# Low parts of queries and keys on GpSimd from SBUF, two GpSimd additions and four denominator groups a half, scratch laid out in tiles

## Chip, core and metric

The kernel runs on one core of a Trainium2 chip. The metric is the device time of one execution in microseconds, as the median of several runs. The engines are TensorE (PE in the profile, its weight loads PEld), VectorE (DVE), ScalarE (ACT), GpSimd (POOL) and SyncE (SP, which only issues DMAs here).

## What is computed

A gated block: attention of the normalised `x` over a context that is both keys and values, added to `x` through a gate, and then a feed-forward part with values rounded to 16 bits and weights to 4.

```python
q = q * cos + rotate_half(q) * sin            # q = layernorm(x), k = v = ctx_1024
k = k * cos + rotate_half(k) * sin            # B, T, H = 4, 1024, 512; 16 heads of 32
bias = alibi_slopes(nh)[:, None, None] * rel.astype(q.dtype)
scores = jnp.einsum('bqhd,bkhd->bhqk', q, k) * scale + bias[None]
out = jnp.einsum('bhqk,bkhd->bqhd', jax.nn.softmax(scores, axis=-1), v)
...
x = act_qdq(x)                                # rounds by one scale for the whole tensor
up = act_qdq(x @ lpbq_dequant(w_up).T)        # w_gate, w_up: (1536, 512); w_down: (512, 1536)
gate = act_qdq(x @ lpbq_dequant(w_gate).T)
gate = act_qdq(gate * fixed_qdq_u16(jax.nn.sigmoid(gate)))
o = act_qdq(gate * up)
return o @ lpbq_dequant(w_down).T
...
x = x + jnp.tanh(g_xattn[0]) * _L0_xattn_ref(_layernorm(x), ctx_1024, ctx_1024, 16)
x = x + jnp.tanh(g_ffn[0]) * _L0_ffn_ref(_layernorm(x), w_gate, w_up, w_down)
```

## The kernel before

The program is written out engine by engine: each engine has a function that issues its instructions in a fixed order, and semaphores tie the engines together. `STEPS`, a list of `Step` objects, is the order of the attention for all five engines; nothing is scheduled by a tool.

**Attention.** Four heads of one batch are worked on at a time, 16 such quads. A quad has two halves of 512 queries (`hf`, 0 to 31), and a half has eight steps (`s`), one for each 128 keys. In this text `w` is 8 times the half in its quad plus `s`, 0 to 15, and `p` is the quad. In each step:

- TensorE computes the scores of four heads (`score`, L934), the scores of ten steps later once more in the other direction to find row maxima (`row_max`, L921), and the products of the exponentials of the step before with the values (L983). Each is four matmuls side by side in the array, one for each 32 columns.
- ScalarE takes the exponentials of four heads (L1145), out of two PSUM banks in turn, so TensorE can be only two heads ahead. They go to `Pb`, a ring of `NP` = 6 buffers. Between them, or behind them in the step, ScalarE has `numT` (step 1, L1176), `denT` (step 3, L1182), high parts (L1123), normalised tiles (L1095), and later weights.
- VectorE reduces two score tiles of 1024 columns to row maxima (L1348), out of two double banks (`quad`) in turn. The order of their uses is `UNIT_USES`: a use waits until that of two places before is read.
- GpSimd rotates queries and keys (`rope`, L1781 to L1799, three parts in three steps) and adds exponentials.

**Denominators.** The sum over keys is made of eight tiles of exponentials. In each half GpSimd adds tiles 0 and 1, tiles 3 and 4, and tiles 6 and 7 (`sum`, L1936) into `Ps[0]`, `Ps[2]` and `Ps[1]`; two DMAs that accumulate, issued by GpSimd, add tile 2 to `Ps[0]` and tile 5 to `Ps[2]` (`accumulate`, L1915). TensorE multiplies the three sums with ones (`denominators`, L956): group 0 in step 6, groups 1 and 2 in steps 1 and 2 of the next half. The last half is done otherwise: VectorE adds pairs, and there are four groups.

**Low parts.** Queries and keys are split into two half-precision numbers each. ScalarE writes the high part into `S` from the rotated `t1`. For the low part ScalarE copies `t1` into a bank of `quad` (`copy_part`, L1129), which is one more use of these, and VectorE subtracts the high part from it (`low_part`, L1367) at `w` = 1, 6, 10 and 14. When both are there, SyncE issues a transposing DMA (`load_stack`) into `QA` or `KA`.

**Feed-forward part.** Gate and up projections run on TensorE; ScalarE copies each tile of 128 x 1024 out of PSUM, and SyncE stores it into `gate_scratch` or `up_scratch` in HBM, laid out (12, 128, 4096) (L784). They are loaded back when the scale of the whole tensor is known: `load_gate` for the gate beside the up projection, `load_product` for the maximum of the product after it, and `load_o` in halves of 512 columns beside the down projection.

Of the kernel before, what the change touches and what calls it, by code (L numbers as in the profile page):

```python
# [15 lines left out]
N = B * T  # L16
# [12 lines left out]
NXL, NWL, NWQ, NP = 7, 4, 2, 6  # L29
# [86 lines left out]
class Step:  # L116


    def __init__(self, g):
# [109 lines left out]
def unit_uses():  # L229

    uses = []
    for st in STEPS:
# [4 lines left out]
        if st.low is not None:  # L237
            uses.append(("part", *st.low))
# [25 lines left out]
def den_no(hf, n):  # L264

    return 3 * hf + n + 1


def sum_no(hf, n):

    return 3 * hf + (1, 3, 2)[n]
# [56 lines left out]
class Kernel:  # L328


    def __init__(self, nc, ctx, x, ctx_in, gx, gf, wg, wu, wd, cos_d, sin_d, id_d, bias_d, out):
# [9 lines left out]
        self.gate_d = nc.dram_tensor("gate_scratch", (OT, 128, N), F32).ap()  # L341
        self.up_d = nc.dram_tensor("up_scratch", (OT, 128, N), F32).ap()
# [45 lines left out]
        self.Pb = [A(f"P{i}", [128, 4, 512], F32) for i in range(NP - 1)]  # L388
        self.bias = nc.alloc_sbuf_tensor_at("bias", [32, T], F32, offset=A.at - 2 * 8192)
        self.biasT = A("biasT", [128, 8, 4, 16], F16)  # L390
        self.Ps = [A(f"Ps{i}", [128, 4, 512], F32) for i in range(3)]
# [32 lines left out]
        self.Pb.append(A("P5", [128, 4, 512], F32))  # L424
# [87 lines left out]
        self.a_cp = sem("a_cp")  # L512
# [10 lines left out]
    def bank_release(self, use, half):  # L523

        n = UNIT[use] - 2
        while n >= 0:
# [3 lines left out]
            if kind == "out":  # L530
                return (self.v_x2 if half else self.v_rec), a[0] + 1
            if half == 0:
                return self.v_lo, part_no(*a)
            n -= 2
# [97 lines left out]
def sync_program(e, K):  # L632
# [22 lines left out]
    def load_stack(p, w, half):  # L655
# [10 lines left out]
        e.wait_ge(K.v_lo, part_no(p, w, half))  # L666
# [113 lines left out]
    def store_projection(n, dst_d):  # L780
# [3 lines left out]
        e.dma_start(dst_d[ot, :, 1024 * cp:1024 * cp + 1024], K.ev[k % NEV][:, :]).then_inc(K.d_ev[k % NEV], 16)  # L784
# [31 lines left out]
    def load_gate(n):  # L816
# [5 lines left out]
        e.dma_start(K.gt[n % NGT][:, :], K.gate_d[ot, :, GW * cp:GW * cp + GW]).then_inc(K.d_gt[n % NGT], 16)  # L822
# [26 lines left out]
    def load_up(ot, sl, w):  # L849
# [7 lines left out]
        e.dma_start(K.uf[n % NUF][:, 0:w], K.up_d[ot, :, sl]).then_inc(K.d_uf[n % NUF], 16)  # L857
# [1152 lines left out]
```

## Time and profile before

| | us |
|---|---|
| median of 3 runs | 1798.62 |
| lowest and highest | 1795.56, 1801.59 |
| the profiled execution | 1800.73 |
| its span, first to last instruction | 1798.9 |

| engine | busy us | share of the span |
|---|---|---|
| TensorE | 1605.8 | 89% |
| VectorE | 1479.7 | 82% |
| ScalarE | 1241.8 | 69% |
| GpSimd | 838.6 | 47% |

The attention takes the time up to about 900 us, gate and up projection run until about 1440 us, the maximum of the product is searched until 1547 us, and then the down projection runs to the end.

How to read it: in a timeline a row has the start in us from the first instruction, the duration, the engine, the line, the operation, what it writes and reads, shapes, and how many instructions were merged; brackets give the idle time before it and what ended it. A merged row's duration spans all of it. A product in single precision counts as two matmuls. In the table of stretches each engine has its busy time and, in parentheses, its instructions, in the order PE, PEld, DVE, ACT, POOL; then follow TensorE's granted clock as a share of full speed, the busy share of the DMA engines and GB/s. Busy shares of engines that wait for each other do not add up; what sets the end has to be read from the order of events.

### The profile page before, as it was taken

What the parts mean: (1) busy time and instruction counts of PE and PEld (TensorE: products, weight loads), DVE (VectorE), ACT (ScalarE), POOL (GpSimd) and SP (SyncE); (2) the same over time, 40 slices, a digit from 0 to 9 for tenths busy, and PEclk for the clock granted to TensorE, in tenths of its full rate; (3) what the DMA queues carried; (4) which work ended last, traced back from release to release, by engine and by line L of the source; (5) the groups of instructions that cost most, each with busy time, mean ns of one, the idle gap of its engine ahead of it and who ended that gap; (6) DMA issues with size and microseconds to landing.
All of it is one profiled execution on the core that took longest, in us unless ns stands there. A gap on an engine that the chain in (4) does not pass through costs nothing. (4 is left out here: it accounts for less than half of the span.)

```text
span 1798.9 us, 36886 instructions
## 1 busy us (share of the span) xinstructions
PE 1605.8 (89%) x14777; PEld 633.3 (35%) x14777; DVE 1479.7 (82%) x2116; ACT 1241.8 (69%) x1974; POOL 838.6 (47%) x504
## 2 busy tenths in 40 slices
PE   3899999999999999999869999999999900699999
PEld 0233333333333333333224444444444400344444
DVE  7899999999998898898569989768889998854551
ACT  3688888888889899888723323359986699844440
POOL 5699999999999999998600100200000000000000
PEclk9999999999999999999979999999999955899999
DMA  6688888988888887776649888569973479755551
GB/s 153 151 154 179 167 164 180 177 164 167 163 173 161 171 183 151 163 151 136 139 117 275 242 250 239 203 194 284 280 226 127 139 250 302 237 189 172 176 168 61
DMA packets 344204, 331.73 MB, mean 184 GB/s; under 512 B 214849, under 2 KB 273601, under 8 KB 336097
## 3 DMA queue, kind: packets, MB, share of 16 engines
q1 hardware_dynamic: 335104, 264.37, 55.2%
q0 software_dynamic: 8928, 65.02, 18.3%
q8 instruction: 116, 1.90, 0.4%
q14 instruction: 56, 0.45, 0.1%
HBM read 136.77 MB, written 76.55 MB: 119 GB/s over the span
## 5 line engine op out<-in xcount | busy, mean ns | idle before, releaser
L1348 DVE TENSOR_REDUCE cm<-quad 128x1 f16<-128x1024 f32 x512 | 600.3, 1214 | 63.3 <-PE quad L921 62.3
L1145 ACT ACTIVATE P<-quad 128x512 f32<-128x512 f32 x1024 | 556.8, 598 | 112.3 <-PE quad L934 100.5
L1936 POOL TENSOR_TENSOR Ps<-P,P 128x2048 f32<-128x2048 f32 x93 | 441.0, 4742 | 43.2 <-ACT P L1145 43.1
L934 PE MATMUL quad<-QA,KA 101*32 101x512 f16 x4096 | 365.9, 385 | 6.8 <-ACT P L1145 5.3
L921 PE MATMUL quad<-KA,QA 100*32 100x512 f16 x4096 | 334.7, 391 | 35.6 <-DMA QA<-S 17.8
L983 PE MATMUL quad<-P,cg 128*32 128x512 f32 x2048 | 265.5, 594 | 0.0
L1010 PE MATMUL quad<-x_hl,Wu 128*128 128x512 f16 x1152 | 250.8, 381 | 3.4 <-DMA Wu<-wt_scratch 3.4
L1010 PE MATMUL quad<-x_hl,Wg 128*128 128x512 f16 x1152 | 249.3, 379 | 3.1 <-DMA x_hl<-xs 2.5
L1063 PE MATMUL quad<-Wd,oh 128*128 128x512 f16 x768 | 228.6, 379 | 0.0
L934 PEld LDWEIGHTS quad<-QA,KA 101*32 101x32 f16 x4096 | 105.0, 94 | 298.6 <-ACT P L1145 231.0
L1226 ACT ACTIVATE ev<-quad 128x1024 f32<-128x1024 f32 x96 | 97.3, 1014 | 123.4 <-PE quad L1010 117.3
L921 PEld LDWEIGHTS quad<-KA,QA 100*32 100x32 f16 x4096 | 106.4, 96 | 176.1 <-DVE cm L1348 78.2
L1010 PEld LDWEIGHTS quad<-x_hl,Wu 128*128 128x128 f16 x1152 | 113.0, 98 | 141.0 <-DMA Wu<-wt_scratch 4.3
L1010 PEld LDWEIGHTS quad<-x_hl,Wg 128*128 128x128 f16 x1152 | 112.4, 98 | 140.0 <-issue 5.0
L1618 DVE TENSOR_REDUCE mxt<-ev 128x1 f32<-128x1024 f32 x96 | 116.5, 1214 | 39.6 <-ACT ev L1226 39.3
L1063 PE MATMUL quad<-Wd,ol 128*128 128x512 f16 x384 | 145.5, 379 | 0.0
L1883 POOL TENSOR_TENSOR wq<-wl,wsc 128x512 f32<-128x512 f32 x36 | 43.9, 1221 | 216.5 <-DVE wl L1486 216.5
L1257 ACT ACTIVATE sgm<-gq,qs 128x1024 f32<-128x1024 int16 x96 | 110.0, 1147 | 38.1 <-DVE sgq L1663 36.6
L956 PE MATMUL quad<-Ps,ones 128*32 128x512 f32 x776 | 101.9, 600 | 17.1 <-POOL Ps L1936 7.2
L1759 DVE SCALAR_TENSOR_TENSOR xr<-quad,qs,xr 128x512 f32<-128x512 f32 x32 | 23.9, 750 | 112.3 <-PE quad L1063 108.0
L1063 PEld LDWEIGHTS quad<-Wd,oh 128*128 128x128 f16 x768 | 75.1, 98 | 90.7 <-DVE ol L1738 0.2
L1016 PE MATMUL quad<-ident,column 128*128 128x128 f32 x3 | 1.4, 457 | 110.9 <-DVE column L1421 110.9
(167 smaller groups left out, 2006.3 us busy)
## 6 DMA issues: line engine op xcount, KB each, us to landing
Ps<-P POOLq DMA_DIRECT2D x62, 1024.0 KB, 8.1
gate_scratch<-ev SPq DMA_DIRECT2D x48, 512.0 KB, 3.8
gt<-gate_scratch SPq DMA_DIRECT2D x48, 512.0 KB, 5.8
up_scratch<-ev SPq DMA_DIRECT2D x48, 512.0 KB, 3.4
uf<-up_scratch SPq DMA_DIRECT2D x48, 512.0 KB, 5.1
uf<-up_scratch SPq DMA_DIRECT2D x96, 256.0 KB, 3.6
wt_scratch<-wh SPq DMA_DIRECT2D x72, 128.0 KB, 2.8
xl<-in_x_dram SPq DMA_DIRECT2D x32, 256.0 KB, 5.1
```

Of the source, the lines that this page charges most:

```text
L921: mm = e.matmul(K.bank(use, c)[j:j + 32, :], K.QA[p % 2][0:100, 4 * qc + qt, h, j:j + 32], K.KA[p % 2][0:100, 4 * c:4 * c + 4, h, :], star ...
L934: mm = e.matmul(K.score[h % 2][j:j + 32, :], K.KA[p % 2][0:101, kt, h, j:j + 32], K.QA[p % 2][0:101, 4 * qc:4 * qc + 4, h, :], start=True, ...
L956: mm = e.matmul(K.den[32 * h:32 * h + 32, :], K.ones[:, :], K.Ps[n % 2 if hf == NHALF - 1 else n][:, h, :], start=n == 0, stop=n == (3 if ...
L983: mm = e.matmul(K.num[32 * h:32 * h + 32, :], K.cg[(p + 1) % 4][:, kt, 32 * h:32 * h + 32], K.Pb[before.g % NP][:, h, :], start=kt == 0, s ...
L1010: mm = e.matmul(K.quad[z][:, 512 * h:512 * h + 512], W(part, c), K.x_hl[:, x, c0:c0 + 512], start=n == 0, stop=n == 11)
L1063: mm = e.matmul(ps, o[k][:, ot, sl], K.Wd[r][:, ot, :], start=ot == m == 0, stop=ot == OT - 1 and m == 2)
L1145: e.activation(K.Pb[pb][:, h, :], K.score[h % 2], ACT.Exp, scale=SCALE / (QPOW * KPOW)).then_inc(K.a_exp, 1)
L1226: e.activation(K.ev[k % NEV][:, :], K.quad[k % 4][:, :], ACT.Copy).then_inc(K.a_ev, 1)
L1257: e.activation(K.sgm[n % NSG][:, :], view(n), ACT.Sigmoid, scale=sg).then_inc(K.a_sig, 1)
L1348: e.tensor_reduce(cm[:, col:col + 1], K.quad[UNIT["max", hm, u] % 2][:, :], AX.X, ALU.max).then_inc(K.v_max, 1)
L1618: e.tensor_reduce(K.mxt[:, col:col + 1], K.ev[k % NEV][:, :], AX.X, ALU.max, apply_absolute_value=True).then_inc(K.v_mx, 1)
L1936: e.tensor_tensor(K.Ps[n][:, :, :], K.Pb[(st.g - 1) % NP][:, :, :], K.Pb[st.g % NP][:, :, :], ALU.add).then_inc(K.g_sum, 1)
```

## The change

- The low parts of quads 1 to 15 are subtracted by GpSimd, from `t1` and `S` in SBUF. ScalarE's copy and VectorE's subtraction go, and the use of a `quad` bank with them. They stand at `w` = 1, 7, 11 and 15.
- GpSimd adds tiles 0 and 1 and tiles 3 and 4. Tiles 6 and 7 are not added: TensorE reads them as groups of their own. Group 0 (`Ps[0]`) stands in step 6, groups 1 and 2 (tiles 6 and 7) in step 7 and in step 0 of the next half, group 3 (`Ps[1]`) in its step 2.
- `Pb` has seven buffers, since tiles 6 and 7 are read later; `Ps` has two.
- `gate_scratch` and `up_scratch` are laid out (12, 4, 128, 1024), so a tile is one contiguous piece.

```diff
-NXL, NWL, NWQ, NP = 7, 4, 2, 6
+NXL, NWL, NWQ, NP = 7, 4, 2, 7
...
-            elif w in ((10, 14) if p >= 0 else (14, 15)):
-                self.low = (p + 2, 1, w // (14 if p >= 0 else 15))
+            elif w in ((11, 15) if p >= 0 else (14, 15)):
+                self.low = (p + 2, 1, w // 15)
...
-            if w in (1, 6):
-                self.low = (p + 1, 0, w // 6)
+            if w in (1, 7):
+                self.low = (p + 1, 0, w // 7)
...
-        self.sum = (hf, s // 2) if last and s % 2 == 1 else (hf, {1: 0, 4: 2, 7: 1}[s]) if inside and s % 3 == 1 else None
+        self.sum = (hf, s // 2) if last and s % 2 == 1 else (hf, s // 4) if inside and s in (1, 4) else None
...
-        if s == 6 and inside:
-            self.dens = (hf, 0)
-        elif s in (1, 2) and 1 <= hf < NHALF:
-            self.dens = (hf - 1, s)
+        if s in (6, 7) and inside:
+            self.dens = (hf, s - 6)
+        elif s in (0, 2) and 1 <= hf < NHALF:
+            self.dens = (hf - 1, 2 + s // 2)
...
-        if st.low is not None:
-            uses.append(("part", *st.low))
...
-        self.gate_d = nc.dram_tensor("gate_scratch", (OT, 128, N), F32).ap()
-        self.up_d = nc.dram_tensor("up_scratch", (OT, 128, N), F32).ap()
+        self.gate_d = nc.dram_tensor("gate_scratch", (OT, N // GW, 128, GW), F32).ap()
+        self.up_d = nc.dram_tensor("up_scratch", (OT, N // GW, 128, GW), F32).ap()
...
-        else:
-            if n == 1:
-                e.wait_ge(K.g_sum, sum_no(hf, n))
-            else:
-                e.wait_ge(K.d_acc[n // 2], 16 * hf + 16)
+            src = K.Ps[n % 2]
+        elif n in (1, 2):
+            e.wait_ge(K.a_exp, score_no(hf, n + 5, 3))
+            src = K.Pb[(8 * hf + n + 5) % NP]
+        else:
+            e.wait_ge(K.d_acc[n // 3], 16 * hf + 16)
+            src = K.Ps[n // 3]
...
-    def copy_part(p, w, half):
-        use = ("part", p, w, half)
-        e.wait_ge(K.g_rope, rope_no(p, w))
-        e.wait_ge(*K.bank_release(use, 0))
-        e.activation(K.bank(use, 0), K.t1[w][:, 4 * half:4 * half + 4, :].rearrange("t i c -> t (i c)"), ACT.Copy).then_inc(K.a_cp, 1)
...
+    def low_part(p, w, half):
+        rows = slice(4 * half, 4 * half + 4)
+        dst = K.S[w][:, rows, :, :, :].rearrange("t i h n d -> t (i h) n d")
+        src = K.t1[w][:, rows, :].rearrange("t i (h d) -> t (i h) d", d=HD)
+        e.wait_ge(K.g_rope, rope_no(p, w))
+        e.wait_ge(K.d_st[w][half], stack_no(p - 1))
+        e.wait_ge(K.a_hi, part_no(p, w, half))
+        e.tensor_tensor(dst[:, :, 2 - w, :], src, dst[:, :, 0, :], ALU.subtract).then_inc(K.g_lo, 1)
...
-            e.wait_ge(K.g_sum, sum_no(hf, 2 * n))
-            e.dma_start(K.Ps[2 * n][:, :, :], K.Pb[(8 * hf + kt) % NP][:, :, :], accum_op=ALU.add).then_inc(K.d_acc[n], 16)
+            e.wait_ge(K.g_sum, sum_no(hf, n))
+            e.dma_start(K.Ps[n][:, :, :], K.Pb[(8 * hf + kt) % NP][:, :, :], accum_op=ALU.add).then_inc(K.d_acc[n], 16)
+        if st.low is not None:
+            low_part(*st.low)
...
-        e.dma_start(dst_d[ot, :, 1024 * cp:1024 * cp + 1024], K.ev[k % NEV][:, :]).then_inc(K.d_ev[k % NEV], 16)
+        e.dma_start(dst_d[ot, cp, :, :], K.ev[k % NEV][:, :]).then_inc(K.d_ev[k % NEV], 16)
```

TensorE from the end of step 7 to step 2 of the next half, before. L956 is a group of denominators, L934 scores, L921 row maxima, L983 values; the digit behind a name is the buffer, so `Ps1_99` is `Ps[1]`, and one row of x4 is one group:

```order
L983 MATMUL quad3<-P3_94,cg2_86 32x512 x4
L934 MATMUL quad2<-QA1_88,KA1_90 32x512 x8
...
L934 MATMUL quad2<-QA1_88,KA1_90 32x512 x4
L956 MATMUL quad3<-Ps1_99,ones_77 32x512 x4
L983 MATMUL quad3<-P4_95,cg2_86 32x512 x4
L934 MATMUL quad2<-QA1_88,KA1_90 32x512 x8
...
L983 MATMUL quad3<-P5_142,cg2_86 32x512 x4
L956 MATMUL quad3<-Ps2_100,ones_77 32x512 x4
```

and with the change, from step 6 to step 2:

```order
L988 MATMUL quad3<-P1_92,cg2_86 32x512 x4
L961 MATMUL quad3<-Ps0_98,ones_77 32x512 x4
...
L988 MATMUL quad3<-P2_93,cg2_86 32x512 x4
L961 MATMUL quad3<-P2_93,ones_77 32x512 x4
...
L988 MATMUL quad3<-P3_94,cg2_86 32x512 x4
L961 MATMUL quad3<-P3_94,ones_77 32x512 x4
...
L988 MATMUL quad3<-P4_95,cg2_86 32x512 x4
L937 MATMUL quad2<-QA1_88,KA1_90 32x512 x8
...
L988 MATMUL quad3<-P5_142,cg2_86 32x512 x4
L961 MATMUL quad3<-Ps1_99,ones_77 32x512 x4
```

Groups that read `P2` and `P3`, the tiles 6 and 7 of this half, now follow the values in steps 7 and 0, and step 1 has none any more.

GpSimd from the last part of a rotation (step 6) to the first accumulating DMA of the next half, before:

```order
L1799 TENSOR_TENSOR t10_136<-t10_136,t2_138 128x1024
L1936 TENSOR_TENSOR Ps1_99<-P0_91,P1_92 128x2048
L1781 TENSOR_TENSOR t11_137<-cg0_84,cos_75 128x1024
L1936 TENSOR_TENSOR Ps0_98<-P2_93,P3_94 128x2048
L1788 TENSOR_TENSOR t2_138<-cg0_84,sin_76 128x32x16
L1789 TENSOR_TENSOR t2_138<-cg0_84,sin_76 128x32x16
L1915 DMA Ps0_98<-P4_95 128x2048
```

and with the change (L1803 is the low part, `S1` of keys, `S0` of queries):

```order
L1794 TENSOR_TENSOR t10_136<-t10_136,t2_138 128x1024
L1803 TENSOR_TENSOR S1_140<-t11_137,S1_140 128x16x32
L1776 TENSOR_TENSOR t11_137<-cg0_84,cos_75 128x1024
L1803 TENSOR_TENSOR S0_139<-t10_136,S0_139 128x16x32
L1942 TENSOR_TENSOR Ps0_98<-P3_94,P4_95 128x2048
L1783 TENSOR_TENSOR t2_138<-cg0_84,sin_76 128x32x16
L1784 TENSOR_TENSOR t2_138<-cg0_84,sin_76 128x32x16
L1919 DMA Ps0_98<-P5_142 128x2048
```

The sum of 2048 elements between two parts of rotations is gone, and low parts of 512 stand before and behind the first part.

## Rows read from the trace of the kernel before

**Rows 1.** Stretches of time: length, then busy us (x instructions) by engine, clock, DMA.

```profile
200.00:400.00 200.00, 194.44 (x2664) 68.46 (x2664) 187.80 (x263) 172.35 (x322) 187.35 (x107) 1.00 0.84 168
600.00:800.00 200.00, 191.84 (x2616) 67.21 (x2608) 176.10 (x235) 179.11 (x338) 200.00 (x99) 1.00 0.79 161
1200.00:1300.00 100.00, 100.00 (x465) 45.37 (x464) 83.81 (x118) 90.36 (x87) 0.00 (x0) 1.00 0.92 276
```

**Rows 2.** Timeline of ScalarE: start us, duration us, instruction; three `numT` copies.

```profile
113.64 0.71 ACT L1176 ACTIVATE numT<-quad,tg 128x512 f32<-128x512 f32 x1
...
833.31 0.69 ACT L1176 ACTIVATE numT<-quad,tg 128x512 f32<-128x512 f32 x1
...
884.07 0.69 ACT L1176 ACTIVATE numT<-quad,tg 128x512 f32<-128x512 f32 x1
```

**Rows 3.** Timeline of TensorE in halves 10 and 11; in brackets: idle before, and releaser.

```profile
326.24 1.06 PE L956 MATMUL quad<-Ps,ones 128*32 128x512 f32 x8 [0.47 <-POOL Ps L1936]
...
334.18 0.78 PE L934 MATMUL quad<-QA,KA 101*32 101x512 f16 x8
...
338.08 0.61 PE L934 MATMUL quad<-QA,KA 101*32 101x512 f16 x8
...
340.76 0.60 PE L934 MATMUL quad<-QA,KA 101*32 101x512 f16 x8
...
343.43 1.04 PE L956 MATMUL quad<-Ps,ones 128*32 128x512 f32 x8
344.28 0.62 PE L934 MATMUL quad<-QA,KA 101*32 101x512 f16 x8
...
348.52 0.40 PE L921 MATMUL quad<-KA,QA 100*32 100x512 f16 x4 [0.25 <-DVE cm L1348]
```

**Rows 4.** Waits (us, times) before denominator matmuls; landing of the accumulating DMAs, from their lines.

```profile
  DMA Ps<-P: 7.1, 9
...
DMA to landing us min/median/max: 6.8/8.1/10.9
```

**Rows 5.** Timeline of ScalarE, then of VectorE, around two steps 1.

```profile
323.28 1.06 ACT L1123 ACTIVATE S<-t 128x1024 f16<-128x1024 f32 x1
324.23 1.08 ACT L1145 ACTIVATE P<-quad 128x512 f32<-128x512 f32 x2
...
350.71 1.08 ACT L1145 ACTIVATE P<-quad 128x512 f32<-128x512 f32 x2
...
353.20 1.09 ACT L1123 ACTIVATE S<-t 128x1024 f16<-128x1024 f32 x1
...
348.97 2.35 DVE L1348 TENSOR_REDUCE cm<-quad 128x1 f16<-128x1024 f32 x2
351.23 0.68 DVE L1556 TENSOR_REDUCE rmn<-x2s 128x4 f32<-128x512 f32 x1
```

**Rows 6.** Groups by line and form: count, busy us and mean ns, idle before.

```profile
L1367 DVE SCALAR_TENSOR_TENSOR S<-quad,S 128x512 f16<-128x512 f32 x60 | 41.3, 688 | 4.5 <-ACT quad L1129 3.6
...
L1129 ACT ACTIVATE quad<-t 128x512 f32<-128x512 f32 x60 | 36.8, 613 | 17.6 <-DVE cm L1348 17.6
...
L1889 POOL TENSOR_TENSOR wh<-wq,wh 128x512 f16<-128x512 f32 x12 | 20.2, 1686 | 0.0
```

**Rows 7.** Timeline of GpSimd from sum 0 to its accumulating DMA.

```profile
354.20 4.64 POOL L1936 TENSOR_TENSOR Ps<-P,P 128x2048 f32<-128x2048 f32 x1
358.80 1.28 POOL L1788 TENSOR_TENSOR t<-xn,sin 128x512 f32<-128x512 f32 x1
...
361.27 0.76 POOL L1915 DMA_DIRECT2D Ps<-P  x1
```

**Rows 8.** Waits from 1450 to 1545 us; then DMA issues: count, KB, us to landing.

```profile
ACT oh L1296 <- DMA uf<-up_scratch: 5.2, 6, 1.7
...
uf<-up_scratch SPq DMA_DIRECT2D x96, 256.0 KB, 3.6
...
xr<-x_scratch SPq DMA_DIRECT2D x32, 256.0 KB, 3.0
```

More of the change, by code:

```diff
@@ L264, in den_no, with low_no @@
 def den_no(hf, n):
-    return 3 * hf + n + 1
+    return 4 * hf + n + 1
 def sum_no(hf, n):
-    return 3 * hf + (1, 3, 2)[n]
+    return 2 * hf + n + 1
+def low_no(p, w, half):
+    return part_no(p - 1, w, half)
 def rope_no(p, w):
@@ L387, in __init__ @@
         self.KA = [A(f"KA{i}", [128, 8, 4, 128], F16) for i in range(2)]
-        self.Pb = [A(f"P{i}", [128, 4, 512], F32) for i in range(NP - 1)]
+        self.Pb = [A(f"P{i}", [128, 4, 512], F32) for i in range(5)]
         self.bias = nc.alloc_sbuf_tensor_at("bias", [32, T], F32, offset=A.at - 2 * 8192)
         self.biasT = A("biasT", [128, 8, 4, 16], F16)
-        self.Ps = [A(f"Ps{i}", [128, 4, 512], F32) for i in range(3)]
+        self.Ps = [A(f"Ps{i}", [128, 4, 512], F32) for i in range(2)]
+        P6 = A("P6", [128, 4, 512], F32)
         self.numT = A("numT", [128, 512], F32)
@@ L525, in bank_release @@
         n = UNIT[use] - 2
-        while n >= 0:
+        if n >= 0:
             kind, *a = UNIT_USES[n]
@@ L529, in bank_release @@
                 return self.v_max, max_no(*a)
[L530 to L534, printed above, removed]
+            return (self.v_x2 if half else self.v_rec), a[0] + 1
         return None
@@ L665, in load_stack @@
         e.wait_ge(K.a_hi, part_no(p, w, half))
-        e.wait_ge(K.v_lo, part_no(p, w, half))
+        if p == 0:
+            e.wait_ge(K.v_lo, part_no(p, w, half))
+        else:
+            e.wait_ge(K.g_lo, low_no(p, w, half))
         rows = slice(4 * half, 4 * half + 4)
@@ L847, in sync_program, with load_up @@
     uf_uses = [0]
-    def load_up(ot, sl, w):
+    def load_up(ot, cp, sl, w):
         n = uf_uses[0]
@@ L949, in denominators @@
             e.wait_ge(K.v_sum, n + 1)
[L950 to L954 removed]
+            src = K.Ps[n % 2]
+        elif n in (1, 2):
+            e.wait_ge(K.a_exp, score_no(hf, n + 5, 3))
+            src = K.Pb[(8 * hf + n + 5) % NP]
+        else:
+            e.wait_ge(K.d_acc[n // 3], 16 * hf + 16)
+            src = K.Ps[n // 3]
         for h in range(4):
[L956 removed]
+            mm = e.matmul(K.den[32 * h:32 * h + 32, :], K.ones[:, :], src[:, h, :], start=n == 0, stop=n == 3)
         mm.then_inc(K.pe_den, 1)
@@ L1138, in exponent @@
             hm, km = m // 8, m % 8
-            if hm < NHALF - 1 and km % 3 < 2:
-                e.wait_ge(K.g_sum, 3 * hm + km // 3 + 1)
+            if hm < NHALF - 1 and km >= 6:
+                e.wait_ge(K.pe_den, den_no(hm, km - 5))
+            elif hm < NHALF - 1 and km % 3 < 2:
+                e.wait_ge(K.g_sum, sum_no(hm, km // 3))
             elif hm < NHALF - 1:
@@ L1178, in scalar_program @@
             hf = st.den_out
-            e.wait_ge(K.pe_den, den_no(hf, 3 if hf == NHALF - 1 else 2))
+            e.wait_ge(K.pe_den, den_no(hf, 3))
             if hf > 0:
@@ L1189, in scalar_program @@
             high_part(*st.high)
-        if st.low is not None:
-            copy_part(*st.low)
         for job in st.side:
@@ L1359, in low_part @@
         e.wait_ge(K.a_hi, part_no(p, w, half))
-        if p > 0:
-            e.wait_ge(K.d_st[w][half], stack_no(p - 1))
         dst = K.S[w][:, rows, :, :, :].rearrange("t i h n d -> t (i h) n d")
         src = K.t1[w][:, rows, :].rearrange("t i (h d) -> t (i h) d", d=HD)
-        if p > 0:
-            e.wait_ge(K.a_cp, part_no(p - 1, w, half))
-            src = K.bank(("part", p, w, half), 0).rearrange("t (g d) -> t g d", d=HD)
         e.scalar_tensor_tensor(dst[:, :, 2 - w, :], src, 1.0, dst[:, :, 0, :], ALU.mult, ALU.subtract).then_inc(K.v_lo, 1)
@@ L1524, in vector_program @@
                 e.tensor_tensor(y, y, K.xg[p % 4][:, 4 * qc:4 * qc + 4, :], ALU.add).then_inc(K.v_x2b, 1)
-        if st.low is not None:
-            low_part(*st.low)
         if st.rows is not None:
@@ L1779, in rope @@
             e.wait_ge(K.a_hi, part_no(p - 1, w, 1))
-            e.wait_ge(K.v_lo, part_no(p - 1, w, 1))
+            if p == 1:
+                e.wait_ge(K.v_lo, part_no(0, w, 1))
+            else:
+                e.wait_ge(K.g_lo, low_no(p - 1, w, 1))
             e.tensor_tensor(o1, v, cb, ALU.mult)
```

17 lines of the change are left out of this document (8 added, 9 removed).

## The prediction

> **What bounds the kernel now.** I looked first at the stretches of time in [rows 1]. From 200 to 800 us, in the attention, TensorE is busy 96 to 97% and the other engines are close behind: VectorE 94 and 88%, GpSimd 94 and then 100%. Such shares do not say who sets the pace, so I read the instructions of one half in order. A half is eight steps, and its length is the distance of two `numT` copies: from 113.64 to 833.31 us lie 27 of them, so 26.65 us each, and the two after that take 25.38 us each [rows 2]. [Rows 3] are the starts of TensorE's work through one half. The step whose scores start at 338.08 ends at 340.76: 2.68 us, the shortest distance there is; I call that a plain step. A group of denominator matmuls starts at 343.43 and the next scores at 344.28: 0.85 us. The step from 334.18 to 338.08 holds the transposes of the output and takes 3.90, so 1.22 above a plain one. TensorE alone would thus need 8 x 2.68 + 3 x 0.85 + 1.22 = 25.2 us a half. The half takes 26.65, so **1.45 us a half are waits of TensorE**, and TensorE's own work is the rest. Where they lie: before the denominators of the GpSimd sum (0.47 us at 326.24, GpSimd), before row maxima (0.25 at 348.52, VectorE; there is one such place in most steps after VectorE had more to do than its two reductions) [rows 3]. TensorE also waits for the accumulating DMA, 7.1 us over the 31 halves, 0.23 a half [rows 4].
>
> The feed-forward part is TensorE's too until 1440 us (100% in 1200 to 1300, [rows 1]). Between 1450 and 1540 it is idle and the maximum of the product is found; there the loads of `up_scratch` are waited for, 5.2 us in all [rows 8]. After that TensorE runs the last product without gaps.
>
> **The change, part by part.** *Four denominator groups instead of three.* Each of halves 0 to 30 gets one group more, 0.85 us of TensorE with nothing to lie under, since TensorE is the engine without gaps: 31 x 0.85 = 26.4 us if no wait goes. This is the one certain cost. All other parts can only give back waits, at most 1.45 us a half.
>
> *What moves on TensorE.* Groups stood at steps 6, 1 and 2, and stand at 6, 7, 0 and 2. The wait for the third GpSimd sum goes, since groups 1 and 2 read exponentials that are long done. Group 0.85 at steps 7 and 0 also stands where VectorE falls behind: its statistics and its reductions of 0.68 us lie in steps 6, 7 and 0, and the wait at 348.52 follows them. With 3.53 us a step there (2.68 + 0.85) against VectorE's 2.35 + 0.68 = 3.03 [rows 5], I let those waits go whole, and with them those behind the low part, which VectorE no longer does.
>
> *What step 1 loses.* Its group covered ScalarE's work in that step. In step 1 of every second half ScalarE has four exponentials, the `numT` copy and a high part: from 350.71 to 353.20 (2.49) and then 0.95 for the high part (another starts at 323.28 and what follows it at 324.23), so 3.44 us before the next exponential can start, while TensorE without a group would be ready at 2.68 [rows 5]. The lag of 0.76 is paid by TensorE at its third score group, which needs that exponential. In the other half the high part is not there and the `numT` copy alone pushes the fourth exponential past the next score: 0.17, as the copy of the denominators does in step 3 (334.18 starts eight matmuls that take 0.78 and not 0.61 [rows 3]). Together 0.93 over two halves, **0.46 a half**.
>
> *Low parts on GpSimd.* Removed for each: ScalarE's copy to PSUM (613 ns) and VectorE's 688 ns [rows 6]. Added for each: one GpSimd instruction on 512 elements. No row shows that form; a subtraction with a half-precision output of that size takes 1686 ns [rows 6], the strided multiply of 512 elements 1.28 us, and two of these stand in the 2.47 us from 358.80 to 361.27, 1.24 each [rows 7]. I take 1.3, with 1.1 to 1.7 as bounds. Two of them against one sum of 4.6 us: GpSimd has about 2 us a half less to do, and is no longer full in 600 to 800. It hides whole: the low part of step 1 waits for a high part that ends before step 1 and is done some 1.5 us before the sum behind it may start; the transposes that wait for low parts have four steps to land.
>
> *When denominator group 0 may start.* Sum 0, two rotations and the accumulating DMA stand behind one another on GpSimd: 354.20 to 361.27 is 7.07 us [rows 7]. The sum may start 2.7 after the first exponential of step 1, when the fourth ends (the high part behind it starts at 2.49 [rows 5]); it now starts 3.5 after (354.20 against 350.71), since GpSimd is still busy with a rotation that a sum of the half before held up. So the DMA is issued at 9.8 instead of 10.6 and, with a median of 8.1 [rows 4], lands at 17.9. TensorE comes to group 0 at 2.85 + 3.53 + 2.68 + 3.90 + 2.68 + 2.2 = 17.8 in one half and 18.4 in the other (before, in the half of [rows 3]: 19.2, from 324.23 to 343.43). The group comes 0.8 to 1.4 sooner and the DMA 0.8, so I keep today's wait of 0.23 a half. From both sides: nothing if it lands at its fastest (6.8), 3.0 at its slowest (10.9).
>
> *Sum for the attention.* A half becomes 8 x 2.68 + 4 x 0.85 + 1.22 + 0.46 + 0.23 = 26.75 against 26.65: 27 x 0.10 = 2.7 us, and 0.1 for half 1. The two halves behind 833.31 have no rotations and at 25.38 only 0.2 us of waits to give back, so each grows by 0.7: 1.4. Half 0 has waits enough, and the last half already had four groups. Together +4.2, and +0.5 for waits of the late halves, in which ScalarE has more to do: **+4.7 us**.
>
> *Contiguous scratch.* The same bytes, the same rows of 4 KB a partition in SBUF, the same number of DMAs; only the place in HBM differs. Until 1440 TensorE hides all of it. At 1450 to 1540 at most 5.2 us of waits can go [rows 8]. Loads of 256 KB take 3.6 us from `up_scratch` and 3.0 from `x_scratch`, which is contiguous already [rows 8]; but the first come in bursts, the second singly, so I take little of that: **-0.5 us**, bounds 0 and -5. The Trainium skill ("DMA: Bandwidth & Descriptors", the measured table, row on HBM row pitch) advises contiguous tiles against large power-of-two pitches; its smallest pitch, 512 KiB, still gave 207 GB/s where full rate was 214, and the pitch here is 16 KiB, so by that page the layout brings nothing and the sum is 0.5 higher. No run here shows another pitch yet.
>
> The sum is +4.2. The profiled execution took 1800.7 us (1798.9 from first to last instruction) and would take 1804.9; the median of the runs is 1798.6, so 2.1 lower, and becomes 1802.8.
>
> **Rivals.** *1. The accumulating DMA comes too late (slower).* The place is group 0 at step 6. The margin there is 0 in one half and 0.5 us in the other, since step 1 is shorter. It decides from a landing of 8 us on, and half of today's are longer. If GpSimd is later than I have it (a low part at 1.7, the high part before it late) or the landing grows by 0.5, each half waits 0.5 more: 27 x 0.5 = 13.5, so 1816. For it: nine such waits in the trace of before [rows 4]. Against: GpSimd has less to do. Chance 0.18.
>
> *2. The waits go further than I let them (faster).* If neither the lag at step 1 nor the landing is seen, a half is 8 x 2.68 + 4 x 0.85 + 1.22 = 26.06: 27 x (-0.59) + 1.4 - 0.5 = -15.0, so 1784. For it: in 600 to 800 GpSimd is full [rows 1], and what it holds up is spread over all engines, not all of it in rows that I named. Against: the 0.17 of step 3 is there in every half. Chance 0.22.
>
> *3. The layout pays.* All 5.2 us of waits go, and the attention comes out as above: 1798.6 + 4.7 - 5.2, so 1798. Against: packets of a tile are as long as before on the SBUF side, and the waits may be those of too few buffers. It is the case in which the Trainium skill's advice of the same table row held for 16 KiB as well. Chance 0.1.
>
> **How the numbers follow.** My forecast has 0.5, rival 1 0.18, rival 2 0.22, rival 3 0.1. The forecast's own range is 1797 to 1809 (the bounds of the low part, 0.2 us a half either way on the waits). This kernel can be told from no change at about 0.3%, 5.4 us, so beyond 1793.2 and 1804.0. Of my 0.5, 0.29 lie within, 0.19 above and 0.02 below. Rival 1 is slower, rival 2 faster, rival 3 within. Faster 0.24, same 0.39, slower 0.37. The range leaves out the outer halves of rivals 1 and 2: 1787 to 1814.
>
> **What would show it.** In the profile after: TensorE busy share in 200 to 400 above 97%; no wait of denominator groups for GpSimd; waits for row maxima well under today's; 3.5 us from the first exponential of step 1 to that of step 2 in one half of two; the two halves before the last near 26.1; GpSimd under 95% in 600 to 800; waits of ScalarE for `uf` about as now. I am wrong if halves average below 26.4 (then the waits at step 1 are covered by something that I missed) or above 27.0 (then the landing).

## The result, and the profile after

The changed kernel takes 1832.0 us (median of 4 runs, 1828.2 to 1834.9) against 1799.4 us for the kernel before (1795.6 to 1801.6): a ratio of 1.018, 95% interval 1.0163 to 1.0196. The forecast was 1802.8 us in a range of 1787 to 1814; **it was wrong by 29 us**. The profiled execution took 1834.9 us, its span is 1833.1.

The page of the changed kernel. In the second section each digit or number is one fortieth of the span, 45.8 us; then one group of matmuls (count, busy us and mean ns, idle before and releaser):

```profile
PE   3999999589999999999968999999999920699999
PEclk9999999799999999999988999999999965799999
GB/s 158 152 152 160 166 157 182 70 145 185 168 163 159 156 170 166 177 162 134 105 160 162 261 259 258 220 163 284 306 275 118 138 226 310 249 192 170 167 168 64
...
L988 PE MATMUL quad<-P,cg 128*32 128x512 f32 x2048 | 267.4, 598 | 5.5 <-ACT numT L1177 5.5
```

The eighth slice (321 to 367 us) is unlike all others of the attention: TensorE at 5 tenths, the clock at 7, the DMA traffic at 70 GB/s between 182 and 145. Two of the stretches of [rows 1] read now:

```profile
200.00:400.00 200.00, 172.46 (x2285) 59.28 (x2277) 150.68 (x206) 138.21 (x258) 144.10 (x92) 0.93 0.87 140
600.00:800.00 200.00, 195.16 (x2668) 67.51 (x2660) 166.47 (x215) 169.05 (x316) 180.57 (x109) 1.00 0.84 166
```

From 600 to 800 TensorE is at 98% and GpSimd at 90% (under 95% was forecast). From 200 to 400 TensorE lost 22 us against [rows 1]; the DMA engines count as busy as before (share 0.87 against 0.84) but moved less (140 against 168 GB/s).

I took the distance of `numT` copies half by half, as in [rows 2]. Of the 27 distances that the prediction averages, all are between 26.4 and 30.6 us **except one of 55.6 us**, from the copy at 333.21 us to that at 388.84. What happened at its start, first on SyncE's queue, then on GpSimd (start us, duration us; for a DMA the duration is that of its issue):

```profile
325.84 1.35 SPq L672 DMA_TRANSPOSE KA<-S  x1
331.17 1.21 SPq L638 DMA_DIRECT2D cg<-in_ctx_dram  x1
332.55 37.36 SPq L672 DMA_TRANSPOSE KA<-S  x1
370.02 2.28 SPq L672 DMA_TRANSPOSE QA<-S  x1
```

```profile
320.09 4.64 POOL L1942 TENSOR_TENSOR Ps<-P,P 128x2048 f32<-128x2048 f32 x1
324.68 1.29 POOL L1929 TENSOR_TENSOR x2s<-x2s,xg 128x512 f32<-128x512 f32 x1
325.91 0.82 POOL L1919 DMA_DIRECT2D Ps<-P  x1
```

A transposing DMA is issued at 325.84 and an accumulating one at 325.91. In the kernel before, the same pair stood 1.69 us apart, the accumulating one ahead (GpSimd, then SyncE):

```profile
318.37 0.90 POOL L1915 DMA_DIRECT2D Ps<-P  x1
```

```profile
320.06 2.83 SPq L669 DMA_TRANSPOSE KA<-S  x1
```

There they landed after 8.9 and 9.3 us; in the changed kernel they take 31.1 and 38.5 us. The three further DMAs that are issued up to 342 us land after 28.2 to 39.5 us, where the same three took 7.4 to 8.1 before. The DMA issues from 300 to 375 us (count, KB each, median us to landing):

```profile
Ps<-P POOLq DMA_DIRECT2D x4, 1024.0 KB, 19.7
...
cg<-in_ctx_dram SPq DMA_DIRECT2D x1, 512.0 KB, 38.9
...
KA<-S SPq DMA_TRANSPOSE x2, 39.0
```

Over the whole execution the landing of the accumulating DMAs has the same median as before and another maximum (31.1 us against 10.9 in the last row of [rows 4]):

```profile
DMA to landing us min/median/max: 6.9/8.1/31.1
```

And this is what TensorE does with it (timeline, idle before in brackets), and its clock (stretches, columns as in [rows 1]):

```profile
357.09 1.93 PE L961 MATMUL quad<-Ps,ones 128*32 128x512 f32 x8 [19.42 <-DMA Ps<-P]
...
375.01 1.47 PE L924 MATMUL quad<-KA,QA 100*32 100x512 f16 x12 [4.61 <-issue]
```

```profile
334.00:358.00 24.00, 4.58 (x56) 1.29 (x60) 4.19 (x5) 4.36 (x8) 7.82 (x4) 0.67 1.13 51
358.00:364.00 6.00, 6.00 (x64) 2.15 (x60) 3.14 (x4) 3.00 (x6) 0.00 (x0) 0.61 1.01 103
...
372.00:390.00 18.00, 14.81 (x172) 4.96 (x176) 10.71 (x14) 9.14 (x19) 6.50 (x4) 0.81 1.02 212
```

The long half is 29.2 us above the 26.4 us that the same half takes in experiment 1, and these are they: 19.4 of waiting for the accumulated `Ps` of half 9; 4.6 before row maxima that need a `QA` which SyncE could issue only at 370.02, behind the issue that held its queue for 37.36 us; and about 5, what is left, in which TensorE works at a lower granted clock, 1.00 before the wait and 0.61 and 0.81 in the two stretches behind it (group L961: 1.93 us here, 1.06 in [rows 3]).

### The profile page after: what moved, and what is told of

It is laid out like the page before. It is cut to its first block and busy times, and to the rows that moved or that the text cites. A ratio compares the mean times of both kernels' runs of the same rounds, so it can differ in the third digit from the quotient of the medians.

```text
span 1833.1 us, 37200 instructions
## 1 busy us (share of the span) xinstructions
PE 1631.6 (89%) x15025; PEld 640.8 (35%) x15025; DVE 1448.6 (79%) x2056; ACT 1209.4 (66%) x1914; POOL 765.7 (42%) x533
## 3 DMA queue, kind: packets, MB, share of 16 engines
q8 instruction: 118, 1.93, 0.4%
## 5 line engine op out<-in xcount | busy, mean ns | idle before, releaser
L937 PE MATMUL quad<-QA,KA 101*32 101x512 f16 x4096 | 369.4, 388 | 10.3 <-ACT P L1146 8.9
L924 PE MATMUL quad<-KA,QA 100*32 100x512 f16 x4096 | 325.9, 393 | 30.6 <-DMA QA<-S 18.4
L1942 POOL TENSOR_TENSOR Ps<-P,P 128x2048 f32<-128x2048 f32 x62 | 285.4, 4603 | 128.6 <-ACT P L1146 128.5
L1015 PE MATMUL quad<-x_hl,Wu 128*128 128x512 f16 x1152 | 248.8, 379 | 0.0
L1309 ACT ACTIVATE uq<-uf,qs 128x512 int16<-128x512 f32 x96 | 68.2, 711 | 48.8 <-DMA uf<-up_scratch 46.4
L961 PE MATMUL quad<-Ps,ones 128*32 128x512 f32 x528 | 70.6, 611 | 29.4 <-DMA Ps<-P 24.7
```

The lines of the kernel that those rows point to most:

```text
L924: mm = e.matmul(K.bank(use, c)[j:j + 32, :], K.QA[p % 2][0:100, 4 * qc + qt, h, j:j + 32], K.KA[p % 2][0:100, 4 * c:4 * c + 4, h, :], star ...
L937: mm = e.matmul(K.score[h % 2][j:j + 32, :], K.KA[p % 2][0:101, kt, h, j:j + 32], K.QA[p % 2][0:101, 4 * qc:4 * qc + 4, h, :], start=True, ...
L961: mm = e.matmul(K.den[32 * h:32 * h + 32, :], K.ones[:, :], src[:, h, :], start=n == 0, stop=n == 3)
L1015: mm = e.matmul(K.quad[z][:, 512 * h:512 * h + 512], W(part, c), K.x_hl[:, x, c0:c0 + 512], start=n == 0, stop=n == 11)
L1942: e.tensor_tensor(K.Ps[n][:, :, :], K.Pb[(st.g - 1) % NP][:, :, :], K.Pb[st.g % NP][:, :, :], ALU.add).then_inc(K.g_sum, 1)
```

## Experiments

All ratios are to the kernel before, run beside it on the same chip.

**1. The deviation later.** Ahead of that accumulating DMA GpSimd works through `deviation_2(0)`, some 4 us of small operations. Two steps later it stands behind the DMA.

```
-            if st.g == 16 * p + 12:
+            if st.g == 16 * p + (14 if b == 0 else 12):
```

> The changed kernel with one group of small GpSimd instructions (deviation_2 of batch 0, about 4 us) two steps later, behind the accumulating DMA of half 9 and not ahead of it. Collision theory: in the changed kernel this DMA is issued 70 ns after a transposing DMA (KA<-S) has been issued, everywhere else at least 0.37 us before it, and here alone landings take 28 to 39 us. Issued some 4 us sooner it lands in 7 to 10 us, half 10 takes 27 us and not 55.6, and the kernel takes 1800 to 1805 us. Rival (the seventh buffer, the second queue's load or GpSimd's own speed make landings longer in general, wherever they fall): a stall of the same size stays, here or in another half, and the kernel takes 1825 to 1835.

Measured: **1800.2 us** (10 runs, 1797.7 to 1802.5), ratio 0.9996 (0.9986 to 1.0006), span 1798.3. The long half takes 26.4 us, and the transposing DMA now comes 3.5 us behind the accumulating one. Between the two profiled spans lie 34.8 us, and the one half is 29.2 of them; the rest is spread over other halves, of which the one of 30.6 us, 26.4 here, is the largest. The whole kernel is then no slower than before. This run also gives the attention without the stall: mean half 26.94, last `numT` copy at 916.2 us against 908.1.

**2. Which part of the change makes it?** The old scratch under the changed kernel; the low parts alone; sums and groups alone (the diff's lines of each kind, nothing else).

> The changed kernel with the old layout of gate_scratch and up_scratch. The stall in half 10 stays under every theory (1855 if the layout has no part in it), and the layout's share shows: 1838 to 1842 us if it is worth 7.8 us, 1830 to 1834 if nothing. From the last numT copy to the end 891 us and not 883 in the first case.

> The kernel before with the low parts on GpSimd as its only change: three sums and three denominator groups as before. If relief of VectorE and ScalarE is what the low parts are worth, TensorE's waits for row maxima go and a half gets up to 0.6 us shorter: 1783 to 1790 us. If GpSimd is the bound (it has 26.9 us of work in a late half of 26.9, and the low parts add 2.4), late halves grow to about 29 and early ones to 27.5: 1835 to 1850 us. A collision as in the changed kernel would show as one half of over 50 us.

> The kernel before with two GpSimd sums, four denominator groups and seven buffers as its only change; low parts by ScalarE and VectorE as before. TensorE gets 0.85 us a half more, and step 1, which has no group any more, now has the numT copy, the copy of the low part and a normalised tile uncovered. If TensorE's own work sets the length, a half is 27.2 to 27.6 and the kernel takes 1815 to 1828 us; if GpSimd's relief pays for it, it takes 1795 to 1803.

Measured: old scratch **1847.7 us** (2 runs), ratio 1.0259 (1.0231 to 1.0287): the stall is there with the old layout too (half of 55.3), with a second long half of 32.8. I had expected 1838 to 1842. The attention ends at the same time as in the changed kernel (last copy at 950.0 and 950.1 us), and what comes behind it takes 895.1 us against 883.0, so the layout is worth 12 us in this pair of traces and not 7.8. Low parts alone **1844.4 us**, ratio 1.0257 (1.0201 to 1.0313): a half of 40.3 us at the same place, and beside it halves of 28 to 31 us late in the attention, since GpSimd now has the low parts and all three sums. Its stretch from 600 to 800 us:

```profile
600.00:800.00 200.00, 182.09 (x2432) 63.44 (x2432) 156.96 (x208) 158.16 (x296) 199.04 (x112) 0.97 0.75 150
```

GpSimd is full (199.04) and TensorE at 91%. Groups alone **1816.4 us**, ratio 1.009 (1.0075 to 1.0105): no stall, mean half 27.25, GpSimd at 162.14 there. So either part alone costs more than both together: the last `numT` copy, at 908.1 us before, comes at 927.9 with the groups alone, at 958.6 with the low parts alone (12 to 14 us of it their stall) and at 916.2 with both and no stall. The low parts need the GpSimd time that the third sum gave up. Together they still cost the attention 8.1 us, and it is the scratch that pays for them in the whole kernel. And the stall comes with the low parts: in groups alone the transposing DMA comes 1.36 us behind the accumulating one, in low parts alone 0.05.

**3. Is it lateness, or nearness?** In the kernel before the accumulating DMA came 1.7 us ahead of the transposing one. Spare GpSimd operations whose result nobody reads delay it, nothing else is changed (the runs with five, and the changed kernel with three, multiply `K.ones` and not `K.half`):

```
+        if st.g == 16 * 4 + 14:
+            for i in range(N):
+                step_of(K.spare[:, :], K.half[:, :], K.half[:, :], ALU.mult, K.g_spare, i + 1)
         if st.accumulate is not None:
```

> The kernel before with 8 small GpSimd instructions (about 2.2 us) that nobody reads, ahead of the accumulating DMA of half 9. There it is issued 1.69 us before the transposing DMA KA<-S; now 0.3 to 0.6 us after it. Collision theory: landings of 25 us and more at 318 to 322 us, and 1820 to 1830 us in all. Rival (the stall belongs to what else the changed kernel does): at most 2 us more than before, 1797 to 1803.

> As e3_late_dma with 6 small instructions and not 8. There the accumulating DMA was issued 0.77 us after the transposing DMA KA<-S and nothing happened. In the two runs with the stall it was issued 0.07 and 0.09 us after it. With 6 it should be 0.1 to 0.2 after. If coincidence within a tenth or two of a microsecond makes the stall, landings of about 30 us come and the kernel takes 1826 to 1832; if it takes something else of the changed kernel, 1799 to 1804.

> The kernel before with six spare operations of GpSimd, three of 128x8 and three of 128x4, ahead of the accumulating DMA of the second half of pair 4, nothing else. In the kernel before the transposing DMA was issued 1.69 us behind the accumulating one there; six of 128x8 took that to -0.20 us and eight to -0.77 us, neither with a stall. These six should take it to about -0.1 us (-0.15 to -0.03). Theory (issue within about 0.1 us stalls both, whatever the rest of the kernel does): the transposing DMA and the accumulating one land 20 to 40 us after their issue, one half takes 38 to 56 us, and the time is 1812 to 1832 us. Rival (the stall needs what only the changed kernel does, its low parts or its four groups): landings of 8 to 12 us, no half over 30 us, and 1798 to 1806 us. If the distance comes out beyond 0.15 us to either side, the run tells nothing between them.

> The same as the run before it, but one spare operation of 128x8 and five of 128x4, which should put the two issues at about 0.0 us from each other (-0.05 to +0.08). Theory: as there, a stall of 20 to 40 us in the landing, one half of 38 to 56 us, 1812 to 1832 us. Rival: no half over 30 us, and 1798 to 1806 us. Beyond 0.15 us to either side it tells nothing between them.

> The kernel before with five spare operations of 128x8 ahead of the accumulating DMA of the second half of pair 4, nothing else. The three runs with six came out at -0.20 to -0.23 us (the transposing DMA that far ahead of the accumulating one) without a stall, and one operation is worth 0.26 us in them, so this one should come to about +0.05 us, where the kernel with the low parts alone had its stall. Theory (nearly simultaneous issue stalls both, in any of these kernels): landings of 20 to 40 us, one half of 38 to 56 us, 1812 to 1832 us. Rival (the stall needs what the changed kernel does beside it): landings of 8 to 12 us, no half over 31 us, 1798 to 1806 us.

> The kernel before with five spare operations of 128x16 there, each some 0.02 us longer than one of 128x8: about -0.04 us, close to the -0.07 us of the changed kernel. Theory and rival as for the run before it, with the same numbers; if both runs stay without a stall at less than 0.1 us, the theory of nearness alone falls.

and the same in the changed kernel, one and three operations:

> The changed kernel with one spare 128x8 operation of GpSimd (its result is used by nothing) ahead of the accumulating DMA in the step where the long half began, nothing else. Six such operations moved the issue by 1.9 us in the kernel before, so one moves it by about 0.3 us: the transposing DMA would be issued 0.35 to 0.4 us ahead of the accumulating one and not 0.07. Theory (the two stall each other only when they are issued within about 0.1 us): although GpSimd has more to do and the accumulating DMA comes later, the stall goes, the accumulating DMA lands in 8 to 14 us, the half takes 26 to 30 us, and the time is 1798 to 1806 us. Rival (a late accumulating DMA is the cause, however it stands to the other): the half stays at 55 us or more and the time at 1828 to 1836 us. Second rival (the pair meets in another half instead): a half over 35 us elsewhere, 1815 to 1836 us.

> The changed kernel with three spare operations of 128x8 ahead of the accumulating DMA. One moved it to -0.19 us: a milder stall in the profiled execution (half of 31.9 us, 1811.0 us) and, by its time, the full one in the other (1835.5 us). Three should put it at -0.6 to -0.75 us. Theory (distance decides): landing of 8 to 13 us, half of 26 to 30 us, all runs at 1798 to 1806 us although GpSimd has the most to do here. Rival (it is the load of the changed kernel at that place, and each operation more makes it worse): a half over 35 us, 1828 to 1840 us.

What came, sorted by the distance from the accumulating to the transposing issue in the profiled execution (plus: the transposing one comes later; read from both timelines, as above; landings of the two DMAs; us):

| kernel | distance | `Ps` lands | `KA` lands | longest half | time |
|---|---|---|---|---|---|
| groups alone | +1.36 | 7.7 | 10.1 | 28.2 | 1816.4 |
| low parts alone | +0.05 | 22.9 | 23.8 | 40.3 | 1844.4 |
| before, 5 of 128x8 | +0.04 | 26.0 | 31.8 | 56.6 | 1827.8 and 1799.9 |
| before, 5 of 128x16 | +0.01 | 29.2 | 34.7 | 56.5 | 1830.3 and 1838.6 |
| changed | -0.07 | 31.1 | 38.5 | 55.6 | 1832.0 |
| changed, old scratch | -0.09 | 30.7 | 36.2 | 55.3 | 1847.7 |
| changed, 1 op | -0.19 | 15.2 | 11.8 | 31.9 | 1811.0 and 1835.5 |
| before, 6 ops (three kernels) | -0.20 to -0.23 | 11.0 to 11.2 | 8.5 to 8.8 | 29.6 to 29.7 | 1802.1, 1801.4, 1803.1 |
| before, 8 ops | -0.77 | 10.3 | 5.7 | 28.0 | 1803.6 |
| changed, 3 ops | -1.12 | 10.7 | 4.3 | 28.4 | 1801.7 |

The two kernels with five operations are the kernel before in everything but about 1.6 us of GpSimd time, and they stall. The rows of the second, SyncE then GpSimd then TensorE:

```profile
319.45 2.23 SPq L671 DMA_TRANSPOSE KA<-S  x1
323.04 1.32 SPq L640 DMA_DIRECT2D cg<-in_ctx_dram  x1
324.52 37.31 SPq L671 DMA_TRANSPOSE KA<-S  x1
```

```profile
319.44 0.91 POOL L1920 DMA_DIRECT2D Ps<-P  x1 [0.27 <-issue]
```

```profile
348.68 1.94 PE L958 MATMUL quad<-Ps,ones 128*32 128x512 f32 x8 [13.92 <-DMA Ps<-P]
```

It is the picture of the changed kernel: an issue of 37.31 us, a wait of 13.9. Its ratio is 1.0187 (1.0116 to 1.0258), while six or eight operations, which delay the DMA more, give 1.0010 to 1.0016; and the changed kernel with three operations more is at 1.0017 (1.0004 to 1.0029) and not at 1.018. **Lateness falls, nearness stands**: within 0.1 us of each other the two stall in all five profiled cases, and from 0.2 us on (seen up to 1.3 us in all traces) neither takes more than 11.3 us to land. The changed kernel with one operation, at -0.19, had a mild stall in the profiled execution and, by its time, the full one in the other; the kernel with five of 128x8, at +0.04, took 1827.8 us with the stall and 1799.9 in an execution whose distance is not known. So these few tenths of a microsecond are a matter of chance from one execution to the next. The halves of 29.6 to 29.7 us with six operations are no stall: TensorE waits 2.0 us there for a GpSimd sum that the operations delay, and 0.9 for the DMA.

All five cases are the same pair, in half 9. One meeting lies elsewhere: in the second long half of the changed kernel with the old scratch a transposing DMA of queries is issued 0.22 us ahead of the accumulating one, the two land after 10.0 and 10.5 us, and TensorE waits 3.7 us before row maxima. Whether a meeting within 0.1 us in another half stalls as much no run shows.

The kept traces also answer whether any DMA of SyncE would do. In the 17 of them SyncE issues a plain DMA less than 0.1 us ahead of an accumulating one 24 times. The accumulating one then lands after 10.9 us at most and the plain one after 9.0, so nearness to just any DMA of SyncE is not enough.

My expectations missed often here. Eight operations came out at -0.77, not -0.3 to -0.6, and there was no stall; that is what left only nearness of the theory. Six operations of either size came out at -0.2 and told nothing of the nearer distances (128x4 takes no less than 128x8); the changed kernel with one came to -0.19, not -0.38, and was not freed of the stall; with three it came to -1.12, not -0.6 to -0.75.

**4. The scratch alone.**

```
-        self.up_d = nc.dram_tensor("up_scratch", (OT, 128, N), F32).ap()
+        self.up_d = nc.dram_tensor("up_scratch", (OT, N // GW, 128, GW), F32).ap()
```

and the same for `gate_d`, with their stores and loads.

> The kernel before with the contiguous layout of gate_scratch and up_scratch as its only change. In the changed kernel's trace the time from the end of the attention (last numT copy) to the end is 883.0 us against 890.8 before. If the layout is the cause of these 7.8 us, this kernel takes 1791 to 1793 us; if they come from something else in the changed kernel (where the attention leaves the engines, what it leaves queued), it takes 1798 to 1800. The attention takes as long as before, last numT copy at 908 us.

Measured: **1793.9 us** (6 runs), ratio 0.9959 (0.9944 to 0.9974). The attention is untouched (last copy at 908.4 us), and what comes behind it takes 881.9 us against 890.9. In the other runs kernels with the old scratch have 886 to 895 there, those with the new 881 to 885. Two terms of it can be read. TensorE in 1194 to 1340 us, before and with the new scratch:

```profile
1194.00:1340.00 146.00, 142.64 (x653) 64.04 (x652) 123.40 (x178) 133.52 (x127) 0.00 (x0) 0.99 0.91 271
```

```profile
1194.00:1340.00 146.00, 146.00 (x678) 66.21 (x677) 128.20 (x190) 133.85 (x128) 0.00 (x0) 1.00 0.84 271
```

TensorE lost 3.4 us there, which its group of matmuls puts down to `Wu`, and now none. The whole up projection takes 248.8 us and not 254.2: the other 2 us the kernel before loses at 1334 to 1337 us, behind that wait, where its granted clock is 0.50. And its long wait for the maximum is 3.0 us shorter, before and with the new scratch:

```profile
L1016 PE MATMUL quad<-ident,column 128*128 128x128 f32 x3 | 1.4, 457 | 110.9 <-DVE column L1421 110.9
```

```profile
L1016 PE MATMUL quad<-ident,column 128*128 128x128 f32 x3 | 1.4, 456 | 107.9 <-DVE column L1421 107.9
```

**5. The copy of the numerators ahead of the exponentials.** The page of after shows TensorE waiting 5.5 us for the copy of the numerators. In the changed kernel with the later deviation that copy is moved ahead of exponentials 0 and 1 of its step; then the same move in the kernel before with the new scratch.

```
-        if st.inside:
+        if st.num_out is None and st.inside:
...
             e.activation(K.numT[:, :], K.num, ACT.Copy, scale=K.tg[:, 0:1]).then_inc(K.a_num, 1)
+            if st.inside:
+                exponent(st.hf, st.s, 0)
+                exponent(st.hf, st.s, 1)
```

> The changed kernel with the deviation moved as in e2_deviation and the numT copy of step 1 ahead of the first two exponentials and not behind them. In the changed kernel each half loses 0.36 us before the values of step 1 (TensorE waits for numT) and 0.44 in every second half before the third scores of step 2. If these waits are the difference to my sum, the first goes whole and the second becomes at most 0.3: about 0.4 us a half, so 12 us less than e2_deviation, 1786 to 1790. If the copy ahead of the exponentials only delays them (ScalarE as the bound), it stays at 1798 to 1802.

> The kernel before with the contiguous scratch, and with the copy of the numerators moved ahead of exponentials 0 and 1 in ScalarE's program of each step that has one; sums, groups and low parts as before. With the scratch alone it took 1793.9 us, and TensorE waited 15.6 us in all for that copy in the kernel before. If the gain of the same move in the changed kernel (11.4 us) was that wait, and the old split of sums, groups and low parts is no worse than the new one, this is 1778 to 1788 us, below the 1788.8 us of the changed kernel with the same move. If the new split is what pays once the copy is out of the way, this stays at 1790 to 1796 us.

Measured: changed **1788.8 us** (4 runs), ratio 0.9929 (0.9903 to 0.9955), mean half 26.62 instead of 26.94, and the halves before the last 26.02 instead of 26.39. It is faster than the kernel before and the changed one. On the kernel before **1795.9 us** (10 runs), 0.9978 (0.9968 to 0.9988), no better than the scratch alone. There a group of denominators covers the copy, and moving it delays exponentials: TensorE's scores then wait for ScalarE

```profile
L934 PE MATMUL quad<-QA,KA 101*32 101x512 f16 x3936 | 350.1, 383 | 14.8 <-ACT P L1145 13.4
```

where they waited 6.4 us before. The 15.6 us of waiting for the copy that my expectation starts from are not TensorE's in the kernel before: its value matmuls waited 0.0 us for it, only weight loads did. So with the same move the new split is ahead, 0.9929 against 0.9978. That it beats the scratch alone (0.9959, 0.9944 to 0.9974) is not shown: the intervals overlap, the four runs lie at 1785 and at 1792 to 1793, and the profiled spans are equal (1790.2 and 1790.4 us).

## Why the prediction was wrong

**The step that failed** is "it hides whole" for the low parts on GpSimd. Their price was right: 1.41 us median (1.3 taken), and GpSimd falls to 90%. But I asked only who waits for the instructions behind them, not what the change does to the moments at which DMAs are issued. The transposing DMA of half 9, 1.69 us behind the accumulating one before, is issued 0.07 us ahead of it now, and there the two stall. I counted every instruction on GpSimd's queue and did not set its DMAs beside those of SyncE. The row to look at was in the trace of before, on SyncE at 320.06 us, 6 us ahead of the first of [rows 3].

Both DMAs moved. Counted from the `numT` copy of half 9, the accumulating one went from 19.97 to 20.45 us and the transposing one, which waits for the last scores of the half, from 21.66 to 20.38. With the groups alone they stand at 19.30 and 20.66, so 0.67 and 1.00 us earlier than before; with the low parts beside them the accumulating DMA comes 1.15 us later than that. So most of the way (from +1.36 to -0.07) is theirs, but a look at GpSimd's delay alone would not have found the meeting.

**Rival 1** (the accumulating DMA comes too late) had the sign and the kind of DMA right, and the place and the mechanism wrong. It supposed 0.5 us in each half before group 0 in step 6, from a landing that is a little later. Measured it is one half, before group 3 in step 2, from a landing 22 us later; over the run the median landing is the old 8.1 us. The forecast's own sign, a mean half above 27.0 "then the landing", did come (28.16), but one half made it.

**The sum for the attention** was +4.7 us; without the stall it is 916.2 - 908.1 = +8.1. The forecast had TensorE's own work at 8 x 2.68 + 4 x 0.85 + 1.22 = 26.06; in the changed kernel with the later deviation the eight steps without their waits add up to 26.04. These are starts of TensorE's scores there, of steps 1, 2 and 3, first in a half whose step 1 has no high part on ScalarE, then in one that has:

```profile
598.05 0.61 PE L937 MATMUL quad<-QA,KA 101*32 101x512 f16 x8
...
601.10 0.62 PE L937 MATMUL quad<-QA,KA 101*32 101x512 f16 x8
...
604.62 0.61 PE L937 MATMUL quad<-QA,KA 101*32 101x512 f16 x8
...
624.44 0.61 PE L937 MATMUL quad<-QA,KA 101*32 101x512 f16 x8
...
627.48 0.62 PE L937 MATMUL quad<-QA,KA 101*32 101x512 f16 x8
...
631.44 0.61 PE L937 MATMUL quad<-QA,KA 101*32 101x512 f16 x8
```

Step 1 takes 3.05 and 3.04 us and not 2.68, and step 2 takes 3.52 and 3.96. Over the 27 halves the steps are longer than they are without waits by:

- step 1: 0.36 in every half, before the value matmuls, which wait for the `numT` copy. I had not seen it. I let that copy push only an exponential, while the next values of TensorE follow it directly once no group stands between. Experiment 5 bears it out: 26.39 - 26.02 = 0.37. It is also why the two halves before the last took 26.39 us and not the 26.1 that I gave as a sign.
- step 2: 0.43 in every second half, at the third score group (0.76 forecast), 0.20 a half. Together with step 1 it is 0.56 a half, where the sum had 0.46, which also held 0.17 of another wait in the halves without a high part.
- step 6: 0.22 a half, of which the accumulating DMA, 3.9 us over the run, is the larger part (0.23 forecast for it), and none for GpSimd sums, as forecast.
- step 0: 0.07 a half, waits for row maxima in four halves; they nearly went, as forecast (2.0 us in all). One long step 4 adds 0.04.

26.04 + 0.36 + 0.20 + 0.22 + 0.07 + 0.04 = 26.93, the measured mean of 26.94. The 0.17 that the copy of the denominators costs, which rival 2 holds against itself, is no term beside these: the step of 3.90 us from which the 1.22 comes contains it.

**The scratch** was mis-sized: -0.5 taken, -5 as its bound, -7 measured in experiment 4. The bound held only the waits of ScalarE from 1450 to 1540 us, and these fell from 5.2 to 2.8. The 3.4 us that TensorE waits before that, and the lower clock behind them, I had set at nothing ("until 1440 TensorE hides all of it"), although it waits there for the transposing loads of `Wu` from HBM; their median landing fell from 5.1 to 4.7 us with the new layout. The Trainium skill ("DMA: Bandwidth & Descriptors", "Latency and other measured facts", row on HBM row pitch) begins at a pitch of 512 KiB with 207 GB/s, where 214 is the full rate. Here the measurement decides for 16 KiB: contiguous tiles alone took the 512 KB loads of `gate_scratch` from 5.8 to 5.4 us and of `up_scratch` from 5.1 to 4.4, and the kernel to 0.9959. Rival 3, which let the Trainium skill's advice hold at 16 KiB, was right on the sign and near in size (-5.2), but had the place only in part.

With +8.1 and -7 the changed kernel would have been at 1799.7, and experiment 1 gave 1800.2. The sum erred by 3.4 us in the attention and by 6.5 the other way in the scratch, so that the forecast of 1802.8 lies only some 3 us from the kernel without the stall. That nearness is in part luck.

## What to carry to other kernels

When a change moves instructions on an engine that also issues DMAs, set its issue times beside those of the other queue, over all rounds and not in one: a meeting in one of 31 cost more than all other terms together. When a mean grows, look first whether every round grew or one did. And where a change takes work away from beside a copy, ask what that work had covered, for each instruction that waits for the copy.

## What the runs showed of the hardware

An accumulating DMA of GpSimd (1 MB, 8 KB packets) and a transposing DMA of SyncE issued within 0.1 us of each other both landed after 23 to 39 us instead of 8 to 10, and held SyncE's queue for 18.5 to 37.6 us at its next transposing DMA. It was seen at five such distances, from +0.05 to -0.09 us, in variants of the changed kernel and of the kernel before, always in half 9; in part at -0.19; and at no distance beyond 0.2 us. Plain DMAs of SyncE issued less than 0.1 us ahead of an accumulating one, 24 in the kept traces, did not do it. During it the DMA engines are counted as busy (share above 1.0) and move 51 GB/s. Of the 224 packets of 8 KB in GpSimd's queue from 318 to 360 us, 21 take over 2 us, up to 13.8, where the median elsewhere is 0.6 and the longest 2.2. What in the DMA engines does this is open: the runs show when it comes, not how. The remedy that was tried is to move the issue of one of the two.

TensorE, idle from 337.7 us, had a granted clock of 0.51 in 342 to 358 us, the lower of its two levels (1.2 of 2.4 GHz). It came out of the wait at 357.1 us with 0.50, which it had until 362.6, and was at 1.00 from 363 to 373 us. Around the end of the second wait, of 4.6 us, it was at 0.50 again, from 373.2 to 379.6 us.
